# A recurrent network step on one Trainium2 core: the base path rearranged, and matmuls of 8 columns in place of 32

## The reference, cut to what matters

```python
# L0: a GRU, one cell per time step
gi = x_t @ W_ih + b_ih;  gh = h @ W_hh + b_hh            # 3 gates of 512
r = sigmoid(i_r + h_r);  z = sigmoid(i_z + h_z);  n = tanh(i_n + r * h_n)
h = (1 - z) * n + z * h
# L1: coupled oscillators, one Runge-Kutta step (4 derivatives) per time step
dq = q - q**3 / 3 - p + drive_t + tanh(q) @ coupling.T + bias
dp = EPSILON * (q + ALPHA - BETA * p)
q, p = clip(q + DT/6*(dq1 + 2*dq2 + 2*dq3 + dq4)), clip(p + ...)   # at +-20
```

## Time and profile before

| | us |
|---|---|
| median of 3 runs | 3839.79 (3839.49 to 3839.97) |
| the profiled execution | 3838.92 |
| its span, first to last instruction | 3836.9 |
| PE busy / PEld busy | 3407.9 (89%) / 3162.4 (82%) |
| DVE busy | 2930.1 (76%) |
| POOL busy | 2263.9 (59%) |
| ACT busy | 1755.8 (46%) |
| mean granted TensorE clock | 0.837 |

### The profile page before, as it was taken

One profiled execution on the slowest core, in us unless ns is written; L12 is line 12 of the kernel. 1 busy time (PEld: TensorE's weight loads), 2 busy tenths in 40 slices (PEclk: granted clock), 3 DMA queues, 4 the chain that ended last, 5 costly groups with the idle time before them and its releaser, 6 DMA issues.

```text
span 3836.9 us, 282781 instructions
## 1 busy us (share of the span) xinstructions
PE 3407.9 (89%) x115469; PEld 3162.4 (82%) x115469; DVE 2930.1 (76%) x18656; ACT 1755.8 (46%) x15007; POOL 2263.9 (59%) x8753
## 2 busy tenths in 40 slices
PE   8988888888888888888888888888888888888877
PEld 4478888888888888888888888888888888888863
DVE  2078888888888888788888888888888888887876
ACT  3244444444444444444444444444444444444443
POOL 0056666666666666666666666666666666666641
PEclk9989888888888788788888888888888788888878
DMA  3000000000000000000000000000000000000001
GB/s 121 22 24 1 1 1 1 1 1 1 1 1 1 1 1 1 1 1 1 1 1 1 1 1 1 1 1 1 1 1 1 1 1 1 1 1 1 1 1 44
DMA packets 9325, 23.37 MB, mean 6 GB/s; under 512 B 556, under 2 KB 600, under 8 KB 8792
## 3 DMA queue, kind: packets, MB, share of 16 engines
q1 hardware_dynamic: 8832, 19.92, 1.4%
q10 hardware_dynamic: 88, 0.02, 0.0%
HBM read 15.75 MB, written 4.19 MB: 5 GB/s over the span
## 4 chain that ended last, share of the span: by engine, by line
PE 42%; DVE 26%; ACT 16%; issue 9%; POOL 7%; DVEq 1%; DMA 0%; ACTq 0%
PE psum L1032 24%; PE psum L1012 12%; ACT tpart L509 9%; DVE psum L815 6%; PE psum L984 4%; DVE tpart L766 4%; ACT tfull L511 4%; POOL term L387 3%; POOL sums L391 3%; DVE gates L703 3%; DVE gates L709 3%; DVE phat L819 3%; DVE zdiff L733 2%; DVE cub L799 2%; DVE psum L806 1%
## 5 line engine op out<-in xcount | busy, mean ns | idle before, releaser
L1032 PE MATMUL psum<-tpart,cpl 128*128 128x32 f16 x65536 | 2017.9, 180 | 371.1 <-DVE tpart L766 370.5
L1032 PEld LDWEIGHTS psum<-tpart,cpl 128*128 128x128 f16 x65536 | 1831.0, 98 | 473.2 <-DVE tpart L766 424.3
L1012 PE MATMUL psum<-hpart,whh 128*128 128x32 f16 x49152 | 1509.3, 181 | 8.0 <-DVE hpart L696 8.0
L1012 PEld LDWEIGHTS psum<-hpart,whh 128*128 128x128 f16 x49152 | 1383.6, 99 | 8.9 <-issue 6.2
L509 ACT ACTIVATE tpart<-psum 128x8 f16<-128x8 f32 x4096 | 701.5, 177 | 1073.3 <-DVE psum L815 1023.1
L815 DVE TENSOR_REDUCE psum<-psum 128x8 f32<-128x24 f32 x4096 | 727.1, 189 | 247.6 <-PE psum L1032 144.3
L766 DVE SCALAR_TENSOR_TENSOR tpart<-tfull,tpart 128x8 f16<-128x8 f32 x4098 | 714.6, 178 | 149.1 <-ACT tfull L511 1.8
L511 ACT ACTIVATE tfull<-psum 128x8 f32<-128x8 f32 x4096 | 688.0, 175 | 0.0
L387 POOL TENSOR_TENSOR term<-coef,qhat 128x32 f32<-128x32 f32 (+1 forms) x1536 | 403.6, 263 | 457.5 <-ACT qhat L516 456.9
L806 DVE SCALAR_TENSOR_TENSOR psum<-cub,sums 128x16 f32<-128x16 f32 x1536 | 330.4, 215 | 253.0 <-POOL sums L391 146.5
L391 POOL TENSOR_TENSOR sums<-sums,term 128x32 f32<-128x32 f32 (+1 forms) x1536 | 403.2, 262 | 120.1
(11 more groups left out here) (155 smaller groups left out, 3324.1 us busy)
## 6 DMA issues: line engine op xcount, KB each, us to landing
xrow<-in_x_dram SPq DMA_DIRECT2D x4, 1024.0 KB, 11.3
out_dram<-space SPq DMA_DIRECT2D x16, 256.0 KB, 2.0
wih<-in_L_cond_W_ih_dram SPq DMA_DIRECT2D x3, 1024.0 KB, 9.9
space<-in_L_cond_W_hh_dram SPq DMA_DIRECT2D x1, 3072.0 KB, 18.9
space<-in_L_cond_coupling_dram SPq DMA_DIRECT2D x1, 1024.0 KB, 19.6
xrow<-in_cond_dram SPq DMA_DIRECT2D x1, 1024.0 KB, 4.6
wih<-in_L_cond_Wk_dram SPq DMA_DIRECT2D x1, 1024.0 KB, 5.5
wih<-in_L_cond_Wo_dram SPq DMA_DIRECT2D x1, 1024.0 KB, 7.7
```

The lines of the kernel that those rows point to most:

```text
L1012: mm = pe.matmul(gate_out[part][:, :, :, col:col + B], whh[:, w, k, n * P:(n + 1) * P], copies_in(hpart[:, k, :, :]), start=(col == 0 and ...
L1032: mm = pe.matmul(stage_out[a][:, :, :, col:col + B], cpl[:, w, k, n * P:(n + 1) * P], copies_in(tpart[:, s % 2, k, :, :]), start=(col == 0 ...
```

## The change

- `COPIES` is 1: each coupling and gate matmul moves its 8 columns once.
- Variables are scaled and shifted so that constants fall away: p is kept minus its rest value (`REST`), so there is no `konst`, `udrive`, `negc3`; q1 is kept in the units of the stage sums, so POOL multiplies it directly (one step less); coefficients of the linear part go into the cubic (`LINEAR`).
- The term of q4 in stage 3's base is part of `LINEAR[3]`, so that this base waits for `sums_ready[2]`, an earlier sum of POOL. p's last term is one add on POOL (`pn`), and POOL clips p, not DVE.
- Stage 3's reduces write `qnext` in SBUF. DVE clips it itself and squares it; ACT does neither. ACT makes an unscaled `q1plain` for the output, which POOL adds (`new_x`).
- DVE's order is written out: `sum_z` comes ahead of stage 3's base, and stage 0's base is made at the end of the step before.

```diff
+REST = ALPHA / BETA
+LINEAR = [-3.0 * (1 + 1 / STEP[0]), -3.0, -3.0, -3.0 - 6 / DT]
 
...
-            lin((-1, p4), (-2 / DT, q[0]), (2 / DT, q[1]), (4 / DT, q[2]), (2 / DT, q[3])),
+            lin((-1, p4), (-2 / DT, q[0]), (2 / DT, q[1]), (4 / DT, q[2])),
             pn]
...
-        COPIES = 4
+        COPIES = 1
...
-                    pool.memset(coef[:, src, r, :], sums_of[r][src])
+                    pool.memset(coef[:, src, r, :], sums_of[r][src] * (STEP[3] if src == 1 else 1.0))
...
             def next_drive(v, t_next):
 
                 pool.wait_ge(h_ready, v)
-                pool.tensor_tensor(x1[:, :], xT_all[:, t_next + 1, :, :].rearrange("p k b -> p (k b)"), h[:, :],
+                if t_next >= 2:
+                    pool.wait_ge(x2_ready, t_next - 1)
+                pool.tensor_tensor(x1[:, t_next % 2, :], xT_all[:, t_next + 1, :, :].rearrange("p k b -> p (k b)"), h[:, :],
                                    ALU.add).then_inc(x1_ready, 1)
...
+            def start_sums(v):
+
                 pool.wait_ge(uhat_ready, v)
...
                 pool.wait_ge(phat_ready, v)
                 pool.tensor_tensor(drive0[:, :], uhat[:, :], phat[:, :], ALU.subtract).then_inc(drive0_ready, 1)
-                pool.tensor_tensor(psum_p[:, :, :], coef[:, 0, :, :],
+                pool.tensor_tensor(sums0[:, :, :], coef[:, 0, :, :],
                                    phat[:, :].unsqueeze(1).broadcast_to([P, 4, KB]), ALU.mult).then_inc(psum_p_ready, 1)
                 pool.wait_ge(psum_p_ready, v)
-                pool.tensor_tensor(sums0[:, :, :], psum_p[:, :, :], udrive[:, :, :], ALU.add).then_inc(sums0_ready, 1)
+                pool.tensor_tensor(sums0[:, 0:3, :], sums0[:, 0:3, :],
+                                   uhat[:, :].unsqueeze(1).broadcast_to([P, 3, KB]), ALU.add).then_inc(sums0_ready, 1)
+
+            def new_x(t):
+
+                pool.wait_ge(q1plain_ready, t + 1)
+                pool.tensor_tensor(xT[:, t, :, :].rearrange("p k b -> p (k b)"), x1[:, t % 2, :], q1plain[:, :],
+                                   ALU.add).then_inc(x2_ready, 1)
...
@@ -373,35 +375,38 @@
                 now, tail = t + 1, t + 2
 
                 pool.wait_ge(q1_ready, now)
-                pool.tensor_tensor(qhat[:, 0, :], q1[:, :], scol[:, :], ALU.mult).then_inc(qhat_ready[0], 1)
-                pool.wait_ge(qhat_ready[0], now)
                 pool.tensor_tensor(term[:, :, :], coef[:, 1, :, :],
-                                   qhat[:, 0, :].unsqueeze(1).broadcast_to([P, 4, KB]), ALU.mult).then_inc(term_ready[0], 1)
+                                   q1[:, :].unsqueeze(1).broadcast_to([P, 4, KB]), ALU.mult).then_inc(term_ready[0], 1)
                 pool.wait_ge(sums0_ready, now)
                 pool.wait_ge(term_ready[0], now)
                 pool.tensor_tensor(sums[:, :, :], sums0[:, :, :], term[:, :, :], ALU.add).then_inc(sums_ready[0], 1)
-
-                for s, lo in ((1, 1), (2, 2), (3, 2)):
+                if t >= 1:
+                    new_x(t - 1)
...
+                for s in (1, 2):
...
-                    if s == 1:
-
-                        pool.wait_ge(x2_ready, now)
-                        pool.tensor_tensor(x1keep[:, :], x1[:, :], ones[:, :], ALU.mult).then_inc(x1keep_ready, 1)
-                        pool.wait_ge(x1keep_ready, now)
-                        if tail <= T:
-                            next_drive(tail, now)
+                    if s == 1 and tail <= T:
+                        next_drive(tail, now)
+
                 if tail <= T:
+                    pool.wait_ge(qhat_ready[3], now)
+                    pool.wait_ge(sums_ready[2], now)
+                    pool.tensor_tensor(pn[:, :], sums[:, 3, :], qhat[:, 3, :], ALU.add).then_inc(pn_ready, 1)
+                    pool.wait_ge(pn_ready, now)
+                    pool.tensor_scalar(phat[:, :], pn[:, :], clampc[:, 0:1], clampc[:, 1:2],
+                                       ALU.min, ALU.max).then_inc(phat_ready, 1)
                     start_sums(tail)
...
                         act.wait_ge(stage_sum[s][a], now)
-                        act.activation(tpart[:, (s + 1) % 2, a * HK:(a + 1) * HK, 0, :], qt[:, a, :].rearrange("p (k b) -> p k b", b=B),
+                        arg = qt[:, a, :] if s < 3 else qnext[:, a * HC:(a + 1) * HC]
+                        act.activation(tpart[:, (s + 1) % 2, a * HK:(a + 1) * HK, 0, :], arg.rearrange("p (k b) -> p k b", b=B),
                                        ACT.Tanh, scale=k_stage[s])
-                        act.activation(tfull[:, a * HC:(a + 1) * HC], qt[:, a, :], ACT.Tanh,
+                        act.activation(tfull[:, a * HC:(a + 1) * HC], arg, ACT.Tanh,
...
-                                       scale=k_stage[s]).then_inc(q1raw_ready, 1)
-                        act.activation(sq[:, 0, :].rearrange("p (a c) -> p a c", a=HALVES), qt, ACT.Square,
-                                       scale=k_stage[s]).then_inc(sq_ready[0], 1)
                         if gru < T:
                             h_high(gru + 1, gru)
+                        act.wait_ge(q1_ready, tail)
+                        if t >= 1:
+                            act.wait_ge(x2_ready, t)
+                        act.activation(q1plain[:, :], q1[:, :], ACT.Copy, scale=k_sixth).then_inc(q1plain_ready, 1)
                     if s == 1 and gru <= T:
                         gate_input(gru, tail)
...
+            def square(v):
+
+                dve.wait_ge(q1_ready, v)
+                dve.scalar_tensor_tensor(sq[:, 0, :], q1[:, :], kap[:, 5:6], q1[:, :],
+                                         ALU.mult, ALU.mult).then_inc(sq_ready[0], 1)
+
...
                 if s == 0:
-                    if not first:
-                        dve.wait_ge(q1raw_ready, t)
-                        dve.tensor_scalar(q1[:, :], q1raw[:, :], CLAMP, -CLAMP, ALU.min, ALU.max).then_inc(q1_ready, 1)
...
-                    dve.wait_ge(sq_ready[0], now)
-                    dve.tensor_scalar(sqkept[:, :], sq[:, 0, :], CLAMP * CLAMP, -3.0 * (1 + 1 / STEP[0]),
-                                      ALU.min, ALU.add).then_inc(sqkept_ready, 1)
-                    if not first and gated_step:
-
-                        h_low(gru)
-
-                    dve.wait_ge(drive0_ready, now)
-                    dve.wait_ge(sqkept_ready, now)
-                    dve.tensor_tensor(cub[:, :], sqkept[:, :], q1[:, :], ALU.mult).then_inc(cub_ready[0], 1)
-                    dve.wait_ge(cub_ready[0], now)
-                    dve.scalar_tensor_tensor(stage_base, in_halves(cub[:, :]), negc3[:, :], in_halves(drive0[:, :]),
+                    dve.wait_ge(sq_ready[0], v)
+                    dve.scalar_tensor_tensor(cub[:, :], sq[:, 0, :], LINEAR[0], q1[:, :],
+                                             ALU.add, ALU.mult).then_inc(cub_ready[0], 1)
+                else:
+                    dve.wait_ge(qhat_ready[s], v)
+                    dve.scalar_tensor_tensor(in_halves(cub[:, :]), in_halves(sq[:, s, :]), LINEAR[s], qt,
...
+            def base(s, v):
+
+                dve.wait_ge(cub_ready[s], v)
+                if s == 0:
+                    dve.wait_ge(drive0_ready, v)
+                    dve.scalar_tensor_tensor(stage_base, in_halves(cub[:, :]), -STEP[3] / 3, in_halves(drive0[:, :]),
                                              ALU.mult, ALU.add).then_inc(base_ready[0], 1)
...
+                    dve.wait_ge(sums_ready[s - 1], v)
                     dve.scalar_tensor_tensor(stage_base, in_halves(cub[:, :]), -STEP[s - 1] / 3, in_halves(sums[:, s - 1, :]),
                                              ALU.mult, ALU.add).then_inc(base_ready[s], 1)
-                    if s == 2 and gated_step:
-                        sum_nr(gru)
-                    if s == 3 and gated_step:
-                        sum_z(gru)
-                dve.wait_ge(base_ready[s], now)
-                for a in range(HALVES):
-                    dve.wait_ge(stage_mm[s][a], now)
-                    dve.tensor_reduce(qt[:, a, :], stage3[a].rearrange("p s c -> p c s")[:, 0:HC, :],
-                                      AX.X, ALU.add).then_inc(stage_sum[s][a], 1)
-                    if s == 3 and a == 0:
-
-                        dve.tensor_scalar(phat[:, :], sums[:, 3, :], clampc[:, 0:1], clampc[:, 1:2],
-                                          ALU.min, ALU.max).then_inc(phat_ready, 1)
-
-                if s == 0:
-
-                    dve.tensor_tensor(xT_all[:, t, :, :].rearrange("p k b -> p (k b)"), x1keep[:, :], q1[:, :],
-                                      ALU.add).then_inc(x2_ready, 1)
-                if s == 2 and gated_step:
+
+            def sum_stage(s, a, v):
+
+                dve.wait_ge(base_ready[s], v)
+                dve.wait_ge(stage_mm[s][a], v)
+                dve.tensor_reduce(qt[:, a, :] if s < 3 else qnext[:, a * HC:(a + 1) * HC],
```

(39 more changed lines are left out.)

125 lines of the change are left out of this document (61 added, 64 removed).

## The result

The changed kernel takes 3923.09 us (median of 4 runs, 3920.79 to 3923.97) against 3839.88 before: ratio 1.0212, 95% interval 1.02 to 1.0224. It is 83 us slower, where 3745 was forecast. One execution of before, disturbed, took 4562 us and is left out of the ratio. The profiled execution of after took 3923.58, its span 3920.7.

What follows compares the result with a forecast made beforehand. PE is neither simply full nor waiting, with real waits of 0.16 and 0.88 us a step. Six groups of 0.853 plus stage 3's 1.52 give 6.638 us against 6.821: 3745 us; own range 3720 to 3775, with rivals 3605 to 3790.

Steps and rivals of the forecast that it cites:

- The clock: PE's granted clock over the whole loop: taken to be 0.50 with 8 columns, from 0.83 before.
- the pace of a group: Each matmul group on PE at the lower clock: 0.853 us, with a lower bound of 0.803.
- stage 3's reduce: End of stage 3: reduce starts 0.80 us after its group, for 0.92 before, no longer waiting for POOL's third sum.
- The start of the step: Stage 0: reduce at 0.94 us, next coupling group possible at 1.67, hidden by 0.04 under two groups of 1.71.
- The end of stage 3: Last coupling group to next step: 0.80 to the reduce plus 0.73 to PE, at most 0.02 less, 1.52 us.
- the +0.03 that was kept as a bound: Reading qnext from SBUF at the end of stage 3: counted as nothing, bounds -0.02 and +0.03 us.
- The first group: First group of a step: 0.853 us, with the second low part of tanh ending about 0.18 after PE's start.
- The fifth rival: Stage 0's base comes late behind waits in a row after a late tanh; slower, 3879 us at reduce 1.24; 7%.
- The second and third rivals: Second: clock 0.50 but groups of 0.803, 3614 us, 10%. Third: clock follows time in flight, 3685 or 3614 us, 8%.
- the fourth: Stage 3's reduce stays 0.92 us behind its group, difference and sum_z being ahead of the base: 3843 us, 6%.
- the sixth: Groups on PE take twice as long at the lower clock: step 12.0 us, some 6480 us in all, 1%.

Runs made afterwards that it cites:

- e1: Changed kernel with 32 columns moved as before (COPIES = 4), so the base path alone: 3841.33 us, ratio 0.9997 to the kernel before.
- e3: Changed kernel, 8 columns, with q's clip bounds and the square's factor as numbers instead of read from tiles: 3851.1 us, ratio 1.0026.
- e7: Changed kernel, 8 columns, with one added wait holding POOL's first term until stage 0's base is written: 3848.46 us, ratio 1.002.
- e5: Changed kernel, 8 columns, with POOL waiting for stage 0's base and q's clip and square constants as numbers: 3825.37 us, ratio 0.9959.
- e9: The kernel of e8 with 8 columns instead of 32: 3809.85 us, ratio 0.9935 to the kernel before.
- e8: Changed kernel, 32 columns, POOL waiting for stage 0's base, numbers in q's clip, square, p's clip, new_h behind tanh's first low part: 3672.3 us.

## Why the prediction was wrong

**What held.** The clock (0.50 throughout), the pace of a group at it (0.853), stage 3's reduce (0.80 forecast, 0.78 measured), and with it that POOL's third sum no longer stands on the path. Clock and pace cost what they were said to cost. In the sums below the differences are of means over the 510 steps of after.

**The step that failed is "The start of the step".** It let the square follow the clip by about 0.11 and the low part of h by 0.10, as if both took the 0.16 of their forerunners, and then kept today's 0.73 from the low part to the reduce. Measured were a clip of 0.36 and a square of 0.39, so that the low part started 0.58 after PE, where 0.21 was counted, and the reduce came at 1.16. Stage 1 starts 0.73 behind it: the first two groups take 1.89, not 1.71, where the base was called hidden by 0.04. That is 96 us of the 178 between forecast and result, and 0.02 in the group behind are another 11. A second error went the other way and kept the miss smaller, by luck: the 0.73 from low part to reduce became 0.58. In before the low part of h took 0.33, having started 0.02 behind POOL's L363; in after it takes 0.22. Two things were wrong with the durations of clip and square:

- They were taken from instructions with numbers in them. The diff shows `clampq` and `kap[:, 5:6]`, and before had an instruction of that form, the clip of p at 0.285 (L819). Away from POOL or in the last 0.03 of an instruction of it, bounds in a tile cost the clip 0.12 (`e1` 0.287 against `e3` 0.164), a factor in a tile the square 0.06 (`e7` 0.234 against `e3` 0.169).
- They were taken from places where POOL had nothing wide ahead of it: before's clip of q starts 0.29 into the 0.34 of POOL's L360, and so meets only its end. In after DVE's chain and POOL's sums run on from the new q and the new p at the same time, and they meet: 0.07 more for the clip (0.355) and 0.16 more for the square (0.392). `e7` takes the meetings behind the clip away and nothing else and wins 75 us; `e3` takes the operands away and wins 72; both win 98 (`e5`). They overlap, since each delays the same reduce, and once it is at 0.98 or so the wait is gone. The 80 us that `e5` is still above the forecast are the end of stage 3 (63) and the first group (12), all but a few.

**The end of stage 3** failed in its second half: 0.73 from reduce to PE became 0.85. `new_h` was said to "fit between the reduces and the low part"; beside POOL's L355 it took 0.30 instead of 0.17 and ended 2007.76, and the low part of tanh, queued behind it, came at 2007.68 and let PE start at 2007.90. Also `tanh` from `qnext` in SBUF takes 0.208 where from PSUM it has 0.179, the +0.03 that was kept as a bound. Together 0.125 a step, 64 us. With POOL's clip of p shorter and `new_h` behind the low part 0.067 of it goes (`e5` to `e9`); that the 0.04 left is ACT's is argued from its lengths, no run takes it away. The order of `e8` with POOL held back brings stage 3 to 1.541 at the full clock; forecast for it were 1.50.

**The first group** was to be 0.853 and was 0.91: the second low part of tanh ends 2008.19, 0.29 after PE started on the first half, where 0.18 was counted. The clip stands ahead of it, and with a clip of 0.165 (`e5`) the group takes 0.873. In after this costs nothing by itself, as stage 1 waits for the late reduce whatever the first group takes; its 29 us are part of the 96, and they are what is left of them in `e7`.

The fifth rival, at 7%, had the right place, but not the cause ("waits in a row behind a late tanh" is not what happened), and not the whole. By its own sum a reduce at 1.17 gives a step of 6.638 + 0.19 = 6.83, 3842 us: the late base eats the forecast gain and no more. That after is 83 us slower, and not level, is the end of stage 3 (64 us), the group behind stage 1's start (11) and a few in the others. The second and third rivals fell (the groups are 0.853, the clock 0.50), the fourth as well (the base is early), and the sixth.

**Why the halves do not add.** The columns cost 18 us on the old path, 82 on the new (`e1` to after), 138 on the one of `e8`. On the old path the four groups behind the start of stage 1 grow from means of 0.850, 0.838, 0.837, 0.838 to 0.875 and three of 0.853, +0.07 us a step or 36 us, and the end of stage 3 gives half of it back (1.664 to 1.631). On the new path the same four grow by 0.07 as well, some 37 us; the rest of the 82 is in the first two groups and in stage 3, 0.02 to 0.03 us each, where DVE meets POOL otherwise at the other pace (`new_h` 0.171 in `e1`, 0.281 in after; the clip 0.287 and 0.355). In `e8` the granted clock is 0.98, and its six groups together are 0.257 shorter than those of `e9`, 131 us; stage 3 gives 8.

**What POOL holds up.** The rows above fit one reading. A DVE instruction with two inputs in SBUF that starts soon after one of POOL ends 0.02 to 0.04 after that one: `new_h`, the base and the low part of h in `e3`; `new_h` and the base in after (2009.03 behind POOL's 2008.99). One that is first is not held (the cubic at 2008.62, POOL's at 2008.67), and one that starts late in POOL's is no longer than alone (the low part of h at 2008.48, 0.28 behind POOL's start: 0.22, as in `e5`).

The clip with numbers, which has one input in SBUF, is held as well when it comes second. In most steps of `e8` it starts 0.05 behind POOL's L359 and takes 0.265, where alone it takes 0.16; the mean is in this row:

```profile
L822 DVE TENSOR_SCALAR q<-qnext 128x16 f32<-128x16 f32 x512 | 121.0, 236 | 0.9 <-issue 0.7
```

The Trainium skill (SBUF — State Buffer, Who interferes with whom) has it so: an exclusive lock between DVE and GpSimd, for a DVE instruction in a 2-port mode, or for one with two SBUF inputs against a GpSimd instruction that reads SBUF, and the second to start waits for the whole of the other. The trace agrees, but for two: the clip and the square of after start 0.05 and 0.04 ahead of POOL's instruction, in 450 and 494 of 512 steps, and are held all the same. The clip of `e3`, with numbers, starts the same 0.05 ahead and takes 0.16. So the operand in the tile decides, and the runs show that much. That its read comes first and lets POOL in would explain it; that is argued, and no run here separates it. If it is so, the two faults of the square are one.
